# Two layer norms moved into the stages that use them, block by block

## What is computed

```python
def _layernorm(x, eps=1e-05):
    return (x - mean(x)) / sqrt(var(x) + eps)
# third attention ("a2"): one head, width 128
Q = queries @ Wq + bq; K = keys @ Wk + bk; V = values @ Wv + bv
scores = where(mask == 0, -inf, Q @ K.T / sqrt(128))
context = softmax(scores) @ V
out = layernorm(context) * ln_gamma + ln_beta
x = x + tanh(g_xattn[2]) * out            # queries = _layernorm(x)
# fourth feed-forward ("f3"): channel mixing with a one-token shift
xr = mu_r * x_ + (1 - mu_r) * x_prev; xk = mu_k * x_ + (1 - mu_k) * x_prev
out = sigmoid(xr @ W_r.T) * (square(relu(xk @ W_k.T)) @ W_v.T)
x = x + tanh(g_ffn[3]) * out              # x_ = _layernorm(x)
```

## Time and profile before

| | us |
|---|---|
| median of 3 runs | 5812.44 (5808.93 to 5820.26) |
| profiled execution | 5809.02, of which the span is 5807.2 |
| the norm's block ahead of a2, first DVE to the first load of a2 | 3778.72 to 3803.96 |
| stage a2, first load to the end of its last DVE work | 3803.96 to 4097.87 |
| the norm's block ahead of f3, first DVE to the first load of f3 | 5723.33 to 5748.49 |
| stage f3, first load to its last update of x | 5748.49 to 5795.13 |

### The profile page before, as it was taken

One profiled execution on the slowest core, in us unless ns is written; L12 is line 12 of the kernel. 1 busy time (PEld: TensorE's weight loads), 2 busy tenths in 40 slices (PEclk: granted clock), 3 DMA queues, 4 the chain that ended last, 5 costly groups with the idle time before them and its releaser, 6 DMA issues. The chain is left out here.

```text
span 5807.2 us, 109944 instructions
## 1 busy us (share of the span) xinstructions
PE 5269.3 (91%) x39878; PEld 3460.8 (60%) x39878; DVE 3857.1 (66%) x10948; ACT 3098.6 (53%) x4492; POOL 1590.2 (27%) x1360
## 2 busy tenths in 40 slices
PE   7999999997959999999999988979458999999996
PEld 4666666665835555555555547857355666666663
DVE  6666666665766666666666667746466666667674
ACT  4666666665624444444444445634145666666664
POOL 3222222221442222222222214500352222222220
PEclk9999999998979999999999989989579999999998
DMA  3333323232233332332332315378333333323230
GB/s 88 77 75 72 79 70 78 68 73 61 62 101 74 81 79 73 81 79 74 83 79 73 77 40 112 74 200 254 84 95 70 75 70 72 74 69 77 68 73 13
DMA packets 160602, 475.40 MB, mean 82 GB/s; under 512 B 34720, under 2 KB 85723, under 8 KB 159866
## 3 DMA queue, kind: packets, MB, share of 16 engines
q1 hardware_dynamic: 148738, 449.69, 32.4%
q0 software_dynamic: 11328, 18.72, 1.1%
HBM read 237.66 MB, written 19.88 MB: 44 GB/s over the span
## 5 line engine op out<-in xcount | busy, mean ns | idle before, releaser
L696 DVE CUSTOM_DVE_ANT_0 a_dump<-a_max,a_mqf 100x482 f32<-100x482 f32 (+1 forms) x1536 | 978.8, 657 | 426.0 <-PE a_max L878 395.0
L1482 DVE CUSTOM_DVE_ANT_0 a_dump<-a_max,a_penq 128x482 f32<-128x482 f32 (+3 forms) x1248 | 783.1, 656 | 403.9 <-PE a_max L1635 382.9
L1475 DVE TENSOR_REDUCE a_mx<-a_max 128x1 f32<-128x482 f32 (+3 forms) x1248 | 779.8, 654 | 397.0 <-PE a_max L1635 273.7
L1635 PE MATMUL a_max<-a_stack,a_qblk 96*128 96x482 f32 (+1 forms) x2304 | 1027.7, 447 | 13.2 <-DVE a_mx L1482 8.5
L562 ACT ACTIVATE a_probs<-a_scores 128x800 f32<-128x800 f32 (+1 forms) x768 | 643.3, 838 | 657.1 <-PE a_scores L895 656.9
L1370 ACT ACTIVATE a_probs<-a_scores,a_kbias 128x800 f32<-128x800 f32 (+1 forms) x768 | 696.9, 926 | 404.2 <-PE a_scores L1662 404.2
L1662 PE MATMUL a_scores<-a_qblk,a_stack 128*128 128x400 f32 (+1 forms) x3072 | 832.2, 353 | 39.9 <-POOL a_qblk L1291 33.3
L1372 ACT ACTIVATE a_probs<-a_scores 128x800 f32<-128x800 f32 (+1 forms) x768 | 624.7, 836 | 410.2 <-PE a_scores L1662 406.1
L878 PE MATMUL a_max<-a_stack,a_qblk 96*100 96x482 f32 (+1 forms) x1536 | 711.1, 483 | 40.5 <-DVE a_mx L696 27.6
L1674 PE MATMUL a_pv<-a_probs,a_v_aug 128*32 128x200 f32 x12288 | 705.7, 341 | 3.0 <-ACT a_probs L1370 2.1
L1662 PEld LDWEIGHTS a_scores<-a_qblk,a_stack 128*128 128x128 f32 (+1 forms) x3072 | 548.1, 184 | 184.6 <-POOL a_qblk L1291 57.2
(11 more groups left out here) (554 smaller groups left out, 8471.2 us busy)
## 6 DMA issues: line engine op xcount, KB each, us to landing
a_stack<-a_khi SPq DMA_DIRECT2D x768, 180.5 KB, 3.4
a_ctxT<-in_ctxT_dram SPq DMA_DIRECT2D x128, 722.0 KB, 11.1
a_stack<-a_klo SPq DMA_DIRECT2D x384, 180.5 KB, 3.5
f_wb<-weights_by_token SPq DMA_DIRECT2D x16, 1600.0 KB
a_ctxn<-in_ctxn_dram SPq DMA_DIRECT2D x32, 704.0 KB
a_mt_i<-in_mask1T_dram SPq DMA_DIRECT2D x32, 600.0 KB, 7.0
a_mq_i<-in_mask_dram SPq DMA_DIRECT2D x32, 564.1 KB
a_mask_i<-in_mask_dram SPq DMA_DIRECT2D x32, 541.5 KB
```

Source lines behind the costliest of these rows:

```text
L696: nc.vector.tensor_tensor_reduce(dump[:, k % 2, 0:n], src, mqf[:, b % 2, o:o + n], 1.0, -3.0e38, ALU.mult, ALU.max, out_).then_inc(mx_free, 1)
L1475: nc.vector.tensor_reduce(out_, src, AX.X, ALU.max).then_inc(mx_free, 1)
L1482: nc.vector.tensor_tensor_reduce(dump[0:rows, k % 2, 0:n], src, penq[0:rows, b % 2, o:o + n], 1.0, -3.0e38, ALU.add, ALU.max, out_).then_i ...
L1635: pe.matmul(to[:, 0:n], qblk[0:96, b % 2, at:at + D], stack[0:96, b % 2, g, o:o + n], start=True, stop=True).then_inc(mx_full, 1)
```

## The change

Both calls of `layernorm_transposed` go. In their place each of the two stages does the same norm within its own block, with statistics of all 32 batches first, then the eight blocks of 4 batches in three functions of the same shape: `normal(n)` on DVE, `x_turn(n)` on PE, `x_out(n)` on ACT. The first two blocks come ahead of everything; the others are placed between the stage's own steps. The loops of the norm and of f3 are written out.

```diff
 # a2, ScalarE
-            act.wait_ge(weights_in, 64)
+            act.wait_ge(in_var_ready, 1)
+            act.activation(tmp[:, 3, :], tmp[:, 0, :], ACT.Sqrt).then_inc(in_root_ready, 1)
+            def x_out(n):
+                act.wait_ge(in_turned, n + 1)
+                act.activation(xnT[:, n * TOK:(n + 1) * TOK], p_t[n % 2][:, 0:TOK], ACT.Copy).then_inc(stored, 1)
...
+            x_out(0)
+            x_out(1)
+            act.wait_ge(weights_in, 64)
             for b in range(3):
                 q_out(b)
                 qk_out(b)
+                x_out(2 * b + 2)
+                x_out(2 * b + 3)
 # a2, VectorE
+            for b in range(B):
+                steps["at"] += 1
+                nc.vector.bn_stats(st[:, b, :], x[:, b, :]).then_inc(dve_step, 1)
+            dve.wait_ge(dve_step, steps["at"])
+            rstd_steps(nc, dve, step, st, mean[:, :], rstd[:, :], tmp, in_var_ready, in_root_ready, 1e-5)
+            def normal(n):
+                if n >= 2:
+                    dve.wait_ge(in_turned, n - 1)
+                for b in range(n * BLK, (n + 1) * BLK):
+                    nc.vector.tensor_scalar(xn[:, n % 2, b % BLK, :], x[:, b, :], mean[:, b:b + 1], rstd[:, b:b + 1],
+                                            ALU.subtract, ALU.mult).then_inc(xn_ready, 1)
+            normal(0)
+            normal(1)
+            normal(2)
+            normal(3)
             penalty(0)
+            normal(4)
+            normal(5)
             penalty(1)
+            normal(6)
+            normal(7)
             for k in range(NCH):
                 mask_scores(0, k)
 # a2, TensorE
-            pe.wait_ge(weights_in, 64)
+            def x_turn(n):
+                if n >= 2:
+                    pe.wait_ge(stored, n - 1)
+                for j in range(BLK):
+                    pe.wait_ge(xn_ready, n * BLK + j + 1)
+                    ins = pe.transpose(p_t[n % 2][:, j * S:(j + 1) * S], xn[:, n % 2, j, :], ident[0:S, 0:S])
+                ins.then_inc(in_turned, 1)
...
+            x_turn(0)
+            x_turn(1)
+            pe.wait_ge(weights_in, 64)
+            pe.wait_ge(stored, 1)
             for b in range(3):
                 q_proj(b)
                 qk_proj(b)
+                x_turn(2 * b + 2)
+                x_turn(2 * b + 3)
                 if b == 0:
                     for k in range(NCH):
                         scores(0, k)
+            pe.wait_ge(stored, NBLK)
             for i in range(B + 2):
 # f3, ScalarE (x_out as above, into p_v)
             def previous(n):
+                act.wait_ge(stored, num(n) + 1)
...
+            x_out(0)
+            act.wait_ge(rest_ready, 1)
             previous(batch(0, 0))
+            x_out(1)
             def iteration(n, more):
+                if num(n) + 2 < NBLK:
+                    x_out(num(n) + 2)
                 if more:
                     previous(nxt(n, 1))
                 activate(n)
 # f3, VectorE (statistics and normal as above)
+            normal(0)
+            normal(1)
+            dve.wait_ge(weights_in, 16 * len(loads))
+            dve.wait_ge(zeroed, 1)
             mixed(batch(0, 0))
             def iteration(n, more, first=False):
+                if num(n) + 2 < NBLK:
+                    normal(num(n) + 2)
                 if more:
                     mixed(nxt(n, 1))
                 product(n)
 # f3, TensorE
             def value(n):
                 pe.wait_ge(act_ready, num(n) + 1)
+                pe.wait_ge(stored, min(NBLK, num(n) + 3))
...
+            def x_turn(n):
+                if n >= 2:
+                    pe.wait_ge(stored, n - 1)
+                if n >= 4:
+                    pe.wait_ge(y_ready, n - 3)
+                for j in range(BLK):
+                    pe.wait_ge(xn_ready, n * BLK + j + 1)
+                    ins = pe.transpose(p_v[n % 2][:, j * S:(j + 1) * S], xn[:, n % 2, j, :], ident[0:S, 0:S])
+                ins.then_inc(in_turned, 1)
+            x_turn(0)
+            x_turn(1)
...
             def iteration(n, more, first=False):
+                if num(n) + 2 < NBLK:
+                    x_turn(num(n) + 2)
                 if more:
                     rk(nxt(n, 1))
 # flamingo_kernel
-            layernorm_transposed(nc, "ln_a2", x, xnT, ident)
-            layernorm_transposed(nc, "ln_f3", x, xnT, ident)
```

More of the change, by code:

```diff
@@ L3771, in iteration @@
                     update_x(nxt(n, -1))
[L3773 to L3779 removed]
+            for n in range(NBLK):
+                iteration(batch(0, n), n + 1 < NBLK, first=(n == 0))
             update_x(batch(0, NBLK - 1))
@@ L3814, in iteration @@
                 value(n)
-            iteration(batch(0, 0), True, first=True)
-            iteration(batch(0, 1), True)
-            iteration(batch(0, 2), True)
-            with pe.Fori(0, (NBLK - 4) // 2) as i:
-                iteration(batch(i, 3), True)
-                iteration(batch(i, 4), True)
-            iteration(batch(0, NBLK - 1), False)
+            for n in range(NBLK):
+                iteration(batch(0, n), n + 1 < NBLK, first=(n == 0))
             turn(batch(0, NBLK - 1))
```

49 lines of the change are left out of this document (32 added, 17 removed).

## The result

The changed kernel takes 5791.6 us (median of seven runs, 5790.0 to 5800.7); the kernel before took 5816.0 in the seven runs measured with it (5808.9 to 5820.3). The ratio is 0.9967, 95% interval 0.9957 to 0.9976: faster by 0.33%. The forecast was 5788 in 5776 to 5802, faster. A repetition on another chip, beside the later experiments, gave 0.9964 (0.9950 to 0.9977). The profiled executions are 5809.0 before and 5790.0 after, 19.0 apart.

A forecast was written before the change was run, and what follows sets the result against it. Early a2 was taken as bound by late loads, later a2 by PE, f3 by a DVE-PE chain. Terms -19.0 - 12.0 - 12.5 + 18.9 = -24.6 us, from 5812.4 to 5788, range 5776 to 5802.

The forecast's parts named there:

- part 3: Later laps of a2: early loads clear the backlog, so eleven laps stop losing time to loads; gain 12.0 us.
- part 5: Laps of f3: the norm is laid in line and TensorE's clock falls to 1.2 GHz; loss 18.9 us.
- Part 1: Norm statistics in both stages: written out, 6.29 us instead of 9.55; first normalised batch 3.7 us earlier.
- Part 2: Start of a2: early loads and interleaved norm blocks bring the third batch's scores forward; gain 19.0 us.
- rival C: a2's early laps stay short of data: gain there 0 to 6 us instead of 12, total 5794 to 5800; chance 0.24.
- slack of 7: a2's regular laps: loads take 7.5 to 8.2 us and are needed two laps, 15.2 us, after issue.
- rival E: All a2 laps take 8.8 us because full DMA engines stay at 251 GB/s; total 5820, slower; chance 0.05.
- Part 4: Start of f3: first product 13.5 us after the first normalised batch; gain 12.5 us.
- Loops written out: f3's loops: writing them out gives nothing, as looped and unlooped warm laps are alike.
- B: f3's laps keep the high TensorE clock: loss 9.5 us instead of 18.9, total 5778; chance 0.18.
- D: f3's norm is really hidden, laps as before with no loss; total 5769; chance 0.08.
- A: The forecast itself, all places as summed: 5788 us; chance 0.45.

The follow-up runs named there:

- a2_serial: Changed kernel with all eight a2 norm blocks done first instead of interleaved, loads still sent at the stage's start; ratio to the kernel before 0.9961.
- f3_warm: Changed kernel with TensorE's idle time in f3 filled by needless matmuls, five after each value and six after each turn; ratio to the kernel before 0.9939.
- f3_prev_first: Changed kernel with two ACT calls swapped in f3's laps, previous(n+1) ahead of x_out(n+2); ratio to the kernel before 0.9953.
- f3_ahead: Changed kernel with f3's norm a lap further ahead on DVE, PE and ACT; ratio to the kernel before 0.9932.
- a2_half_mask: Changed kernel loading only the first half of each a2 mask row from the fourth batch on; ratio to the kernel before 0.9943.
- a2_serial_late: Changed kernel with all eight a2 norm blocks first and the stage's loads held until the last batch is normalised; ratio to the kernel before 0.9996.
- a2_only: Changed kernel with f3 and its norm put back as before, only a2's part of the change kept; ratio to the kernel before 0.9967.
- f3_only: Changed kernel with a2 and its norm put back as before, only f3's part of the change kept; ratio to the kernel before 1.0019.

## Why the prediction was right, and where it wasn't

**The total.** 5788 against 5791.6, and -24.6 against -24.4 in the medians of the first comparison. The four places gave -20.9 in the profile: 5.5 less gain in part 3 and 1.7 more loss in part 5, against 2.5 and 1.0 more gain in parts 2 and 4. The time before came out 3.6 above the 5812.4 that the forecast started from, and a2's own spread is 5 us. So the agreement to a few tenths is luck; the sign, the size and three of the four places are not.

**Part 1, statistics: right.** First normalised batch 9.49 after the statistics start, forecast 9.5; in f3 5696.46 to 5705.95, again 9.49.

**Part 2, start of a2: right, 2.5 us too small.** From the statistics' start to the first exponential it took 25.1 (3780.83 to 3805.89), forecast 27.9; the chain is the forecast one, with `normal(6)` and `(7)` ahead of the first masked score. The oversized terms are the PE ones: scores of batch 0 took 3.56, not the cold 4.30, the two turned blocks ahead of them 1.4, not 2.1, and `q(0)` (3792.74) started 0.24 ahead of the second copy (3792.98), not with it. One wait wasn't foreseen, the second batch's scores standing 0.63 for ACT's last copy; it cost less than those gave. a2_serial says what interleaving is worth by itself: 5.2 at the start, which the laps of the changed kernel gave back.

**Part 3, the laps of a2: a gain, but half of the 12.0 forecast, 6.5.** In the other five profiles of this order it was 0.2 to 6.4: their 28 laps took 220.1 to 226.3, against 226.5 before and 213.6 where nothing waits for a load. That is rival C (0 to 6), not the forecast's side of the range. The step that failed is "in by 3811 ... so the backlog is gone when the regular laps start", and with it the slack of 7 us. SyncE had sent the next mask and ctxT off at 3811.24, and the share stayed at 0.96 to 1.00 from 3812 to 3844. The slack was worked out with a load's time alone in the engines (7.5 to 8.2 us), while it queues behind what is outstanding: the five ctxT loads sent from 3811.98 to 3841.90 took 10.7, 13.2, 15.7, 17.9 and 18.1 us to land. The third of them had 14.2 us, not the 15.2 of two laps, from its issue at 3826.68 to 3840.91, where PE was free for its scores; so a slack of 7 was in truth 1.5 short, and the fourth lap stalled. Then PE's clock fell behind the stall (0.90 in the row above), so a wait of 1.6 us made a lap 3.4 longer. The chance of rival E was 0.05; here it didn't decide, but it took one buffer more to bring its mechanism about.

The Trainium skill ("DMA: Bandwidth & Descriptors", Specifications) states about 358 GB/s from HBM for a core. No stretch of 24 us of a2 in these kernels moved more than 280, and those with a share of 1.02 or 1.03 moved 239 to 276. The trace doesn't reach the page's figure, and the measurement decides, as it did in the prediction: by 358 a lap's loads would take, as an estimate, under 6 us, and no lap would have been short of data.

**Part 4, start of f3: right.** First normalised batch to first product 12.7 (5705.95 to 5718.65), forecast 13.5; the gain was 13.5 instead of 12.5, of which 0.3 is the earlier start of the statistics.

**Part 5, laps of f3: right, and its cause is shown.** +20.6 against +18.9. The chain was forecast at 7.6 warm and is 7.21 (f3_warm); the clock was forecast to cost 1.7 a lap and costs 2.50, since in the changed kernel r, k, the turn and the value product all run at 1.2 GHz (r takes 1.70, value 1.52), while in the lap of the earlier trace rows from which I took 4.49 only a part of them did (1.49 and 0.93): there it was 4.49 from r to product, here 5.29. The two errors nearly cancel (9.3 forecast, 9.7 found). f3_prev_first shows ACT's order to be worth 2.3 us a lap, clock included, and f3_ahead that all of the lengthening is position: with the same instructions it is gone.

**Loops written out: nothing.** f3_ahead, written out, has the 4.64 us laps of the looped kernel.

**Rivals.** B fell (clock 0.64 in f3), D fell for this kernel and came true for f3_ahead, E didn't occur. A held in parts 1, 2, 4 and 5, C in part 3; the total came out 2.4 below C's 5794 to 5800, and parts 2 and 4 gave 3.5 more than forecast.

## What to carry to other kernels

Interleaving a stage's preparation with its first blocks pays by what it sends off earlier, so look first at when the loads are issued: here holding them cost 20 us. The order of the compute work at the start was worth 5.2 where the loads then kept up (a2_half_mask against a2_serial), and nothing that could be measured where they didn't. In a lap loop of several in-order engines, preparation for later blocks belongs where each engine already waits, and far enough ahead that nobody in the current lap waits for it; one call two lines too early on ACT was worth 2.3 us a lap, and the idle time that the chain made in TensorE cost 2.5 us a lap in clock. Where the DMA engines show a share of 1 and stalls remain, try fewer loads in flight before more buffers.

## What the runs showed of the hardware

- With the data queue's share at 102% the engines moved 247 GB/s and a load of 722 KB took 26.2 us to land; at 85% they moved 276 and it took 7.3. Each lap's bytes and packets were the same, so the packets themselves took longer at the higher share: 0.30 us against 0.22 on average (the share of 16 engines' 96 us by 5224 and 5855 packets). The two were on different chips. In a2_serial_late a stretch of 24 us at 1.03 (3839 to 3863) still moved 276, so the share alone doesn't give the rate.
- In f3 TensorE's granted clock was 0.64 on average when a lap had two idle stretches of 1.7 and 1.8 us (after), 0.84 with one of up to 2.0 (before), 0.94 with one of 1.6 (f3_ahead), and 1.00 when needless matmuls left 0.6 and 0.5 of the two (f3_warm); the laps were 9.71, 4.64 to 6.40, 4.64 and 7.21. The Trainium skill ("TensorE: Matmul & The Clock Gate", What's actually happening) has it that the throttled state is the default and activity releases it; by these rows the trace agrees, and eleven short needless matmuls a lap gave back 2.5 us.
- The same a2 code took 258.2 to 263.9 us in six executions, its 28 laps 220.0 to 226.3; the five f3 stages in kernels with both stages changed agreed within 0.2. With the other stage changed, the same f3 code differed by 1 to 1.7: in a2_only at its start (38.8 against 37.0 us to the first product), in f3_only in the laps (53.4 against 55.0).
